# Two expert feed-forward stages with 71 and 39 tiles instead of 72 and 40

## The reference, cut to what matters

```
x = x + L0_conv(ln_c(x))            # 2 of 4 expert 3x3 convolutions per image, and a shared 1x1
t = tokens(x)
t = t + L0_ffn(ln_t(t))             # softmax router, top 2 of 8 experts per token
                                    #   y = w2[e] @ (silu(w1[e] @ x) * (w3[e] @ x)), hidden size 341
x = image(t)
x = x + L1_conv(ln_c(x))            # one dynamic 3x3 filter per image and channel
t = tokens(x)
t = t + L1_ffn(ln_t(t))             # softmax router, top 1 of 8, at most 2560 tokens per expert
                                    #   y = w2[e] @ relu(w1[e] @ x + b1[e]) + b2[e], hidden size 512
```

## Time and profile before

| | us |
|---|---|
| median of three runs | 1901.3 |
| profiled execution, its own time | 1906.94 |
| its span, first to last instruction | 1905.1 |
| PE busy in the span | 1669.2 (88%) |
| DVE busy | 1461.4 (77%) |
| POOL busy | 1046.7 (55%) |
| ACT busy | 1013.9 (53%) |

### The profile page before, as it was taken

One profiled execution on the slowest core, in us unless ns is written; L12 is line 12 of the kernel. 1 busy time (PEld: TensorE's weight loads), 2 busy tenths in 40 slices (PEclk: granted clock), 3 DMA queues, 4 the chain that ended last, 5 costly groups with the idle time before them and its releaser, 6 DMA issues.

```text
span 1905.1 us, 39100 instructions
## 1 busy us (share of the span) xinstructions
PE 1669.2 (88%) x9187; PEld 940.5 (49%) x9188; DVE 1461.4 (77%) x5240; ACT 1013.9 (53%) x1725; POOL 1046.7 (55%) x1196
## 2 busy tenths in 40 slices
PE   1699999999996599999999974989999779999957
PEld 1454545454543255555555532556665444444457
DVE  5778888888887577777777756887776668888857
ACT  1436454544543477777777742556555435555524
POOL 2004565656564677777777773366665446666620
PEclk8799999999998799999999995999888979999989
DMA  8601111111112332222222204122210042222146
GB/s 263 204 16 46 43 48 54 48 52 50 51 40 61 103 88 79 80 77 80 80 78 79 70 20 133 55 69 87 71 50 26 22 115 81 80 80 70 30 141 213
DMA packets 180067, 149.09 MB, mean 78 GB/s; under 512 B 19303, under 2 KB 161823, under 8 KB 179961
## 3 DMA queue, kind: packets, MB, share of 16 engines
q1 hardware_dynamic: 153336, 98.05, 18.4%
q0 software_dynamic: 26624, 49.93, 7.8%
HBM read 76.00 MB, written 77.34 MB: 80 GB/s over the span
## 4 chain that ended last, share of the span: by engine, by line
PE 57%; DVE 22%; issue 8%; ACT 5%; DMA 3%; POOL 2%; ACTq 1%; SPq 1%; DVEq 0%; POOLq 0%
PE banks L783 13%; PE banks L785 13%; PE banks L784 12%; PE banks L778 8%; PE banks L998 6%; PE banks L1048 2%; ACT work L1213 2%; DVE small L1537 1%; DVE small L2036 1%; PE banks L1010 1%; DMA wb_h<-ffn_rows 1%; POOL slot_rows L645 1%; ACTq L1212 1%; DVE small L1707 1%; ACT work L1117 1%
## 5 line engine op out<-in xcount | busy, mean ns | idle before, releaser
L666 POOL DMA_INDIRECT ffn_rows<-work x448 | 486.1, 1085 | 235.5 <-issue 166.0
L645 POOL DMA_INDIRECT slot_rows<-work,small x384 | 386.2, 1006 | 272.2 <-issue 141.2
L1924 DVE TENSOR_TENSOR work<-work 128x512 f16<-128x512 f32 x376 | 261.5, 695 | 12.5
L783 PE MATMUL banks<-work,wb_h 128*128 128x512 f16 x648 | 247.5, 382 | 17.7 <-DVE work L1961 13.2
L785 PE MATMUL banks<-work,wb_l 128*128 128x512 f16 x648 | 247.5, 382 | 0.0
L784 PE MATMUL banks<-work,wb_h 128*128 128x512 f16 x648 | 247.4, 382 | 0.0
L778 PE MATMUL banks<-small,work 128*128 128x128 f32 x1216 | 177.9, 284 | 78.7 <-ACT work L1117 45.1
L1940 DVE SCALAR_TENSOR_TENSOR work<-banks,small,work 128x512 f32<-128x512 f32 x216 | 161.5, 748 | 102.6 <-ACT work L1227 102.6
L783 PE MATMUL banks<-work,wa_h 128*128 128x512 f16 x576 | 221.4, 384 | 6.4 <-issue 6.4
L784 PE MATMUL banks<-work,wa_h 128*128 128x512 f16 x576 | 221.1, 384 | 0.0
L785 PE MATMUL banks<-work,wa_l 128*128 128x512 f16 x576 | 221.1, 384 | 0.0
(11 more groups left out here) (339 smaller groups left out, 3152.0 us busy)
## 6 DMA issues: line engine op xcount, KB each, us to landing
wa_l<-slot_rows SPq DMA_DIRECT2D x112, 264.0 KB, 2.8
work<-ffn_rows SPq DMA_DIRECT2D x32, 512.0 KB, 5.2
work<-in_x SPq DMA_DIRECT2D x16, 512.0 KB, 3.2
ffn_rows<-small SPq DMA_DIRECT2D x32, 256.0 KB, 3.8
out_image<-work SPq DMA_DIRECT2D x16, 512.0 KB, 3.1
ffn_rows<-work POOLq DMA_INDIRECT x448, 2.2
slot_rows<-work,small POOLq DMA_INDIRECT x384, 2.3
slot_rows<-small SPq DMA_DIRECT2D x17, 264.0 KB, 3.4
```

Source lines behind the costliest of these rows:

```text
L645: pool_e.indirect_dma_start(slots, bass.IndirectOffsetOnAxis(ap=slot_i[:, row_buffer(p, i, k), tt:tt + 1], axis=0), rows[row_buffer(p, i, ...
L666: pool_e.indirect_dma_start(dst, bass.IndirectOffsetOnAxis(ap=idg[old.v][:, qq, 0:1].bitcast(I32), axis=0), yt[old.u][:, qq, :], None, bou ...
L783: pe.matmul(dst, wh, nh, start=start, stop=False)
L1924: dve.tensor_tensor(gl[i.u][:, j, :], g32[j], gh[i.u][:, j, :], ALU.subtract).then_inc(sem(p + "gl_done"), 1)
```

## The change

`TILES0` becomes 71 and `TILES1` 39: with 32768 pairs, a multiple of 512, the partly filled rests of eight experts can't add up to more than seven tiles above 64, and in D likewise above 32. 71 and 39 aren't multiples of four, so the loops' ends move too.

```diff
-TILES0 = 2 * TOKENS // TILE + E
-TILES1 = TOKENS // TILE + E
+TILES0 = 2 * TOKENS // TILE + E - 1
+TILES1 = TOKENS // TILE + E - 1
...
 def sweep(...):
-    for t in range(n - per, n + behind):
+    for t in range((n // per - 1) * per, n + behind):
         step(Img(t // per, t % per, per))
...
                 with sp.Fori(1, n // 4) as q:
                     for k in range(4):
                         load_tile(Img(q, k, 4))
+                for k in range(n % 4):
+                    load_tile(Img(n // 4, k, 4))
...
             for v in range(4):
-                sp.wait_ge(sem(f"B_scattered{v}"), 16 * QT * TILES0 // 4)
+                sp.wait_ge(sem(f"B_scattered{v}"), 16 * QT * ((TILES0 + 3 - v) // 4))
...
-                sp.wait_ge(sem(f"D_scattered{v}"), 16 * QT * TILES1 // 4)
+                sp.wait_ge(sem(f"D_scattered{v}"), 16 * QT * ((TILES1 + 3 - v) // 4))
...
-                    dve.wait_ge(rows_loaded(i.v), i.w * 16 + 16 * (TILES1 // 4 + 1))
+                    dve.wait_ge(rows_loaded(i.v), i.w * 16 + 16 * ((TILES1 + 3 - i.v) // 4 + 1))
```

## The result

The changed kernel takes 1888.37 us, the median of six runs (1885.65 to 1890.65), against 1901.38 for the kernel before beside it: ratio 0.9929 [0.9916, 0.9942]. Run again later, it took 1887.3 against 1905.13: 0.9910 [0.9897, 0.9923]. So, by the ratios, it is faster by 13.5 us (0.71%) in the one comparison and by 17.1 (0.90%) in the other; the sum of the prediction said 19.05. The first median lies in the upper end of the forecast's range (1876.0 to 1889.5), 6.2 us above its 1882.2 and 0.8 above the first rival's 1887.6. That this comes so near to the sum is in part luck, as the experiments show.

A forecast was written before the change was run, and what follows sets the result against it. PE was taken to bound B and D, and DVE's mask, held by POOL's additions and code waits, to delay PE in C. 6.71 + 6.96 + 2.65 + 2.73 = 19.05 us off 1901.3 gave 1882.2, range 1876.0 to 1889.5.

The forecast's parts named there:

- the first rival: Whole kernel: only the two removed tiles count, C keeps its time behind POOL's additions; 13.67 us less, 1887.6; chance 0.24.
- The two tiles: Stages B and D: one tile less in each saves 6.71 and 6.96 us, as PE sets a tile's time.
- What the tiles issue: B and D: the removed loads, scatters and matmuls are worth nothing beside the tile's own time; zero.
- the straight loads: SP in B and D: three tile loads become straight code, and nothing of this reaches PE; zero.
- the moved small tiles: Small tiles behind `iota_i` and `tab_i` move by 4 or 12 bytes; taken as zero.
- DVE's code of C: C's DVE loop moves by 36 instructions: the second code wait (1.38 us) goes, 0.53 us per jump, five jumps, 2.65 us.
- the prediction's edges: DVE's C loop: an edge of fetched code ten instructions into the pass causes the second wait; the move leaves one edge less.
- The clock in C: PE in C: one of four half-clock stretches goes as a wait gets shorter, 2.73 us less.
- Only the tiles count: Whole kernel: C keeps its time because POOL's additions hold DVE's mask; 13.67 us less, 1887.6; chance 0.24.
- No stretches at all: PE in C: all four half-clock stretches go, 10.92 us, beside tiles and jumps; 1874.1 us; chance 0.14.
- One stretch more: PE in C: one half-clock stretch is added, costing 2.73 us; 1887.7 us; chance 0.10.
- another engine waits for its code: PE's loops in C and D: each of 11 jumps costs 2.85 us, 31.4 in all; 1919 us, slower; chance 0.03.

The follow-up runs named there:

- the fit: Least-squares fit to 142 of the 143 runs, one term per change: B's tile -7.2, D's -6.4, place of DVE's loop -1.9, whole change 15.5 us.
- a quiet clock: Changed kernel plus eight useless matmuls per image in PE's wait ahead of `positions` in C: 1886.02 us; with 92 semaphore instructions on DVE too, 1887.16.
- D alone: Kernel before with 39 tiles in D and the new loop ends, still 72 in B: 1896.63 us, ratio 0.9966 to the kernel before.
- the place undone: Changed kernel plus 92 semaphore-only DVE instructions between B and C, 128 from the loop's old place: 1889.14 us, ratio 0.9924 to the kernel before.

## Why the prediction was right, and where it was not

- **The two tiles** (6.71 and 6.96): right. 13.6 in the fit; the copies' distances in B and in D's straight end are unchanged.
- **What the tiles issue, the straight loads, the moved small tiles** (zero each): the fit's 13.6 against 13.67 leaves no room for a large one in sum, but two small ones stand against each other. In the profiled executions with 71 tiles in B the copies of D lie closer from the loop on, 0.8 us in all, also where D has 40 tiles. And what stands behind D's last copy takes 92.7 to 94.6 us in the nine of them, 91.0 to 93.0 in the five with 72: some 1.7 us more. The sum had neither. Moving DVE's code by 36 instructions brings neither; the causes stay open.
- **DVE's code of C** (2.65): the mechanism is right and went further than forecast, since both waits of a pass went and not one. The value follows from what POOL's hold leaves uncovered, not from the length of the wait, so the second wait added nothing to it. The loop shows it as 2.33 us with a quiet clock; in the run's time the place is worth 1.9 [0.7, 3.1]. That the waits return at 128 instructions fits the prediction's edges if these lie 128 apart; no other move was run.
- **The clock in C** (2.73, "one stretch less"): this is the step that failed. A stretch's price was right for its own image (2.73 forecast, 23.78 - 20.96 = 2.82 after), but the image behind it makes up 0.4, which was already there in the earlier trace rows (1396.16 - 1375.08 = 21.08 across a jump, not 21.52); 2.3 to 2.4 us remain. Nor are the stretches alike: the first of the four before lasted 6.8 us, and the third of the three after 3.4. The profiled pair has 3 against 4. But the count differs between executions: the three profiled with the old place of the loop and C's PE left as it was had 4, 2 and 3, the four with the new one 3, 3, 3 and 2. In time at half clock that is 37.5, 20.5 and 30.7 us against 23.9, 23.9, 23.9 and 13.7. But these executions are no fair draw: the first lay 5.6 us above its kernel's median and the third 2.9, while the one with 13.7 us lay 6.8 below. The place's term of 1.9 as a whole has no room for 2.65 + 2.73 = 5.4. From the granted clock and span of each run the time at half clock is 213.9 us over 66 runs with the old place and 211.9 over 29 with the new (standard errors 0.9 and 1.2): 2 us, not told from nothing, a fifth of a stretch of 10.2 and some 0.5 us of time. I had read a count from one execution as a property of the kernel.
- **The base.** The sum was made against a profiled execution of 1906.94 us, 5.6 above the median, with a C loop of 241.43 us (eleven images). Two other profiled ones with the old place had 237.66 and 237.87. The 7.58 us that the loop lost from profile to profile thus hold about 4 that these two don't have. So the profiled difference of 19.74 met the sum of 19.05 by luck: a high base and 0.7 us more in D than forecast went one way, the 2.5 us behind D's last copy the other.
- **The rivals.** "Only the tiles count" gave 1887.6, and the first median was 1888.4; all runs together put the truth between it and the forecast, with C worth 1.9. "No stretches at all" did not come by this change; with PE's wait filled they vanish, and eleven images lose 4.9 us. "One stretch more" and "another engine waits for its code" did not occur: PE's waits in B and D are as before.

Not settled: why the clock fell after some of PE's waits of about 2 us and not after others, and why the place pays 0 to 2 us in one session's pairs and 3 to 4 in another's. Intervals of some 2 us per pair allow chance. Open too is what 71 tiles in B change in D and behind it.

## What to carry to other kernels

Count what a profiled execution has by accident (here, half-clock stretches at 2.1 to 2.4 us each) in several executions before a term of a sum rests on it; a count from one belongs in the range. Price a wait by what remains once the next hold on its chain is subtracted: 14.4 us of code waits were worth 2. And look for that next hold first, since the same profile rows named POOL's additions, whose move gave 19 us, more than the removal of two tiles.

## What the runs showed of the hardware

- The same DVE loop of 291 instructions was fetched again in every pass (28 packets in the loop, two waits of about 1.4 us at each jump) or not at all (four packets, no wait), by nothing but its place in the instruction stream. 36 instructions that only touch a semaphore removed the fetches, and 92 more, 128 in all, brought them back.
- Stretches at half clock in the C loop start about a whole number of images apart. With the old place it was 64.9 and twice 44.4 us (before), 129.7 (D alone), 44.4 twice (the place undone); with the new one 64.9 twice in three executions and 85.3 in the fourth. So three images apart is common with the new place, but it comes with the old one too.
- Useless matmuls in PE's wait made the program 2.3 [0.9, 3.7] us faster over all runs, as they kept the clock at 2.4 GHz in the C loop.
- A `128x16` operation of DVE with two inputs in SBUF took 2.18 us beside an addition of POOL (2.34 us), and 0.17 alone.
